# A fused attention and expert kernel: TensorE's order around the weighted values, and each value group cut into two halves of the queries

## The reference

```
x = x + attention(layernorm(x), ctx, ctx, length)     # 16 batches, x is [16, 128, 512]
    per head: attn = softmax(SCALE*log(length) * (q^T k)); out = attn v
x = x + experts(layernorm(x))                          # 2048 tokens of 512, 8 experts, 2 chosen
    per token: sum over the two chosen e of w_e * (silu(t w1_e) * (t w3_e)) w2_e
```

## Time and profile before

| | |
|---|---|
| three runs | 1285.31, 1286.80, 1287.75 us; median 1286.8 us |
| profiled execution | span 1285.3 us from first to last instruction; the page gives no other time of it |
| TensorE | 1125.7 us busy (88%) |
| VectorE | 590.4 us busy (46%) |
| ScalarE | 449.9 us busy (35%) |
| GpSimd | 606.7 us busy (47%) |

### The profile page before, as it was taken

How to read it: one execution, slowest core, us unless ns; L and a number is a source line. 1 busy time by engine, 2 the same in 40 slices (tenths; PEclk the granted TensorE clock), 3 DMA queues, 4 the chain that set the end, 5 groups by cost and what they waited for, 6 DMA issues and landing times.

```text
span 1285.3 us, 20411 instructions
## 1 busy us (share of the span) xinstructions
PE 1125.7 (88%) x5561; PEld 472.8 (37%) x5562; DVE 590.4 (46%) x884; ACT 449.9 (35%) x812; POOL 606.7 (47%) x547
## 2 busy tenths in 40 slices
PE   1899999999999999727999999999999999999810
PEld 0223333333333332213555554455455555544300
DVE  5877787877788875131222222222222222222245
ACT  3266666666666666611111111111111111111200
POOL 6434666666666541126504707428281473800045
PEclk9999999999999999958999999999999999999965
DMA  6454555555555441024203305124241333310157
GB/s 181 148 167 141 168 168 168 164 162 158 159 159 165 138 133 45 19 98 159 99 33 131 123 25 196 65 98 163 98 163 33 131 130 123 122 33 33 34 158 259
DMA packets 87243, 158.92 MB, mean 124 GB/s; under 512 B 13696, under 2 KB 52608, under 8 KB 81792
## 3 DMA queue, kind: packets, MB, share of 16 engines
q1 hardware_dynamic: 73728, 90.23, 22.9%
q0 software_dynamic: 12896, 67.12, 14.9%
q10 hardware_dynamic: 576, 1.05, 0.2%
HBM read 107.50 MB, written 50.86 MB: 123 GB/s over the span
## 4 chain that ended last, share of the span: by engine, by line
PE 75%; DVE 8%; DMA 6%; issue 5%; ACT 4%; POOL 2%; SPq 1%; DVEq 0%; POOLq 0%; ACTq 0%; PEldq 0%
PE rows L1048 30%; PE heads_out L1048 15%; PE heads_out L951 7%; PE scores L938 6%; PE rows L924 6%; ACT W L559 3%; DVE nm L682 3%; DMA W<-parts_dram 3%; PE scores L1081 2%; PE misc L1000 2%; DMA U<-expert_out_dram,fidx 1%; PE misc L1021 1%; PE misc L1040 1%; PE misc L977 1%; POOL U L523 1%
## 5 line engine op out<-in xcount | busy, mean ns | idle before, releaser
L1048 PE MATMUL rows<-W,U 128*128 x1776 | 392.1, 381 | 4.6 <-issue 3.0
L559 ACT ACTIVATE W<-scores 128x512 f32<-128x512 f32 x512 | 282.9, 598 | 160.2 <-PE scores L938 155.0
L682 DVE TENSOR_REDUCE nm<-rows 128x2 f32<-128x1024 f32 x256 | 305.5, 1220 | 58.3 <-PE rows L924 41.3
L1048 PEld LDWEIGHTS rows<-W,U 128*128 128x128 bf16 x1776 | 174.5, 98 | 208.9 <-issue 9.7
L1048 PE MATMUL heads_out<-W,U 128*128 x888 | 200.3, 383 | 5.2 <-issue 5.1
L924 PE MATMUL rows<-W,U 96*128 96x512 bf16 x512 | 163.7, 404 | 44.8 <-DMA W<-parts_dram 25.8
L865 DVE TENSOR_TENSOR U<-rows,U 128x512 f32<-128x512 f32 x78 | 53.8, 691 | 318.9 <-ACT U L627 318.9
L938 PE MATMUL scores<-U,W 128*128 128x512 bf16 x512 | 180.3, 387 | 13.9 <-ACT W L559 4.8
L400 POOL TENSOR_TENSOR W<-U,W 128x2048 bf16<-128x2048 f32 x42 | 171.0, 4072 | 7.7 <-POOL W L399 7.7
L627 ACT ACTIVATE U<-rows 128x512 f32<-128x512 f32 x78 | 46.4, 598 | 331.0 <-PE rows L1048 329.9
L951 PE MATMUL heads_out<-W,U 128*32 128x512 f32 x1024 | 138.0, 611 | 0.1
(11 more groups left out here) (144 smaller groups left out, 780.5 us busy)
## 6 DMA issues: line engine op xcount, KB each, us to landing
U<-wpack_dram POOLq DMA_DIRECT2D x42, 1024.0 KB, 5.2
parts_dram<-U SPq DMA_DIRECT2D x32, 384.0 KB, 4.1
U<-parts_dram SPq DMA_DIRECT2D x32, 384.0 KB, 3.9
W<-parts_dram SPq DMA_DIRECT2D x32, 384.0 KB, 5.1
U<-slots_dram SPq DMA_DIRECT2D x39, 256.0 KB, 2.6
expert_out_dram<-U SPq DMA_DIRECT2D x39, 256.0 KB, 2.1
parts_dram<-U SPq DMA_DIRECT2D x32, 256.0 KB, 3.9
stage<-wpack_dram POOLq DMA_DIRECT2D x12, 512.0 KB, 5.3
```

What stands on the lines that cost most here:

```text
L559: s.activation(probs[:, w % 2, j, kk, :], sc[u % 2][:, :], ACT.Exp) \
L682: v.tensor_reduce(nm[:, bb.parity, 2 * k:2 * k + 2], p1[k % 2][:, :].rearrange("p (c k) -> p c k", c=2), AX_X, ALU.max, negate=True).then_ ...
L1048: ins = m.matmul(bank, stat[:, s_part, k, :], W[:, bass.ds(at_w, 512)], start=(k == 0 and n == 0), stop=(k == n_chunks - 1 and n == 2))
```

## The change

`values` takes a fourth argument `qh` and does 256 of the 512 queries: four matmuls of 256 columns. Each former call is two now, and each loads the same stationary blocks. `pv_done` is raised by the second half alone. TensorE's order in half a window is now: score, unit, score, first half of the values, score, unit, score, second half. The small products are at new places between them, and `take_out` stands at other places among ScalarE's exponentials. VectorE writes one more small table (`tile_at`, twice, once in the whole program), whose first column is -1 in place of 0, and one comparison for the expert tiles reads that.

```diff
-                exps(0, range(0, 3))
+                exps(0, range(0, 4))
                 if pv2.within(0, B - 1):      # copies zt
...
-                exps(0, range(3, 6))
+                exps(0, range(4, 8))
+                exps(1, range(0, 1))
                 if pv.within(0, B - 1):
                     take_out(pv, 1)
-                exps(0, range(6, 8))
+                exps(1, range(1, 2))
...
-                exps(1, range(0, 4))
+                exps(1, range(2, 6))
...
-                exps(1, range(4, 8))
-                exps(2, range(6))
+                exps(1, range(6, 8))
+                exps(2, range(8))
+                exps(3, range(0, 1))
                 if full:
                     take_out(b, 0)
-                exps(2, range(6, 8))
-                exps(3, range(0, 5))
+                exps(3, range(1, 5))
...
+                st.step(v.tensor_copy(tile_at[:, :], tio[:, 1, 0:B]))
+                st.step(v.memset(tile_at[:, 0:1], -1.0))
...
-                def values(bb, w, kk):
+                def values(bb, w, kk, qh):
...
+                    cols = slice(256 * qh, 256 * qh + 256)
...
                     for j in range(4):
-                        ins = m.matmul(ob[32 * j:32 * j + 32, :], vt[:, bb.parity, kc, 4 * (w // 2) + j, :],
-                                       probs[:, w % 2, j, kk, :], start=(kc == 0), stop=(kc == 3))
-                    if kk == 1:
+                        ins = m.matmul(ob[32 * j:32 * j + 32, cols], vt[:, bb.parity, kc, 4 * (w // 2) + j, :],
+                                       probs[:, w % 2, j, kk, cols], start=(kc == 0 and qh == 0),
+                                       stop=(kc == 3 and qh == 1))
+                    if kk == 1 and qh == 1:
                         ins.then_inc(S["pv_done"], 1)
...
                 for w in range(4):
-                    for u in range(8):
-                        if u % 2 == 0:
-                            rows_unit(4 * w + u // 2)
+                    for part in range(2):
+                        u = 4 * part
                         if full:
                             score(w, u)
...
+                        rows_unit(4 * w + 2 * part)
+                        if full:
+                            score(w, u + 1)
+                        if (w, part) == (0, 1) and routes:
+                            reader = gates()
+                        if (w, part) == (1, 0) and ahead:
+                            reader = turn_v()
+                        if (w, part) == (1, 1) and behind:
+                            reader = pick_heads()
+                        value_half(w, part, 0)
+                        if full:
+                            score(w, u + 2)
+                        rows_unit(4 * w + 2 * part + 1)
+                        if (w, part) == (3, 0) and ahead:
+                            reader = turn_maxima()
+                        if full:
+                            score(w, u + 3)
+                        if (w, part) == (0, 0) and routes:
+                            reader = turn_z()
+                        if (w, part) == (1, 1) and routes:
+                            reader = ranks()
+                        if (w, part) == (3, 0) and behind:
+                            reader = spread_sums()
+                        value_half(w, part, 1)
```

More of the change, by code:

```diff
@@ L157, in build @@
         tio = sb("tio", [P, 2, T + 1], F32)
+        tile_at = sb("tile_at", [P, B], F32)
         upto = sb("upto", [P, E, E], F32)
@@ L813, in _ @@
             link(v.tensor_tensor(k3, cnt.unsqueeze(2).to_broadcast([P, E, B]),
[L814 removed]
+                                 tile_at[:, :].unsqueeze(1).to_broadcast([P, E, B]), ALU.is_gt))
             link(v.tensor_reduce(tiles, k3, AX_X, ALU.add))
@@ L958, in slot, with turn_z, gates @@
                     (S["m_ready"], b.n + 1) if full else None
+                def turn_z():
+                    pe.wait_ge(S["z_ready"], b.n - 1)
+                    pe.wait_ge(*reader)
+                    for k in range(KD):
+                        ins = m.transpose(misc[:, k * P:(k + 1) * P], z[:, b.parity, k * P:(k + 1) * P], ident[:, :])
+                    ins.then_inc(S["zt_ps"], 1)
+                    return S["zt_ready"], b.n - 1
+                def gates():
+                    pe.wait_ge(*reader)
+                    for k in range(KD):
+                        ins = m.matmul(misc[:, 0:E], zt[:, k, :], gw[:, k, :], start=(k == 0), stop=(k == KD - 1))
+                    ins.then_inc(S["gate_ready"], 1)
+                    return S["gate_used"], b.n - 1
@@ new lines, in turn_v, with pick_heads @@
+                def turn_v():
+                    pe.wait_ge(S["cv_in"], b.n * 16 + 32)
+                    if reader:
+                        pe.wait_ge(*reader)
+                    for kc in range(4):
+                        ins = m.transpose(misc[:, kc * P:(kc + 1) * P], cv[:, kc * P:(kc + 1) * P], ident[:, :])
+                    ins.then_inc(S["vt_ps"], 1)
+                    return S["vt_ready"], b.n + 2
+                def pick_heads():
+                    if reader:
+                        pe.wait_ge(*reader)
+                    pe.wait_ge(S["og_ready"], b.n * 2)
+                    for gr in range(2):
+                        ins = m.matmul(misc[:, :], selu[:, gr, :], og[:, gr, :], start=(gr == 0), stop=(gr == 1))
+                    ins.then_inc(S["u_ready"], 1)
+                    return S["us_ready"], b.n
@@ new lines, in ranks, with turn_maxima @@
+                def ranks():
+                    pe.wait_ge(*reader)
+                    pe.wait_ge(S["mask_ready"], b.n - 1)
+                    m.matmul(misc[:, 0:E], ltri[:, :], maskb[:, :], start=True, stop=False)
+                    m.matmul(misc[:, 0:E], onesb[:, :], mask_sum[:, :], start=False, stop=True) \
+                        .then_inc(S["rank_ready"], 1)
+                    return S["rank_used"], b.n - 1
+                def turn_maxima():
+                    pe.wait_ge(S["p1_used"], b.n * 16 + 32)
+                    if reader:
+                        pe.wait_ge(*reader)
+                    m.transpose(misc[:, 0:P], nm[:, nb.parity, :], ident[:, :]).then_inc(S["mt_ready"], 1)
+                    return S["m_ready"], b.n + 2
@@ new lines, in spread_sums, with value_half @@
+                def spread_sums():
+                    pe.wait_ge(S["rec_in"], b.n * 16)
+                    if reader:
+                        pe.wait_ge(*reader)
+                    m.matmul(misc[:, :], selb[:, :], r8[:, :], start=True, stop=True).then_inc(S["r_ready"], 1)
+                    return S["t_ready"], b.n
+                routes = pv2.within(0, B - 1)
+                def value_half(w, part, qh):
+                    if w == 0 and behind:
+                        values(pv, 3, part, qh)
+                    if w > 0 and full:
+                        values(b, w - 1, part, qh)
```

64 lines of the change are left out of this document (3 added, 61 removed).

## The result

The kernel after takes 1313.76 us (median of four runs, 1312.35 to 1316.07) against 1287.28 for before (1285.31 to 1289.91): a ratio of 1.0204, interval 1.0182 to 1.0225, slower by 26.5 us. The forecast was 1312. One run further down, of dve_late_old, came out slow (1308.94 us, granted clock 0.914 against 0.96 in the others) and its median leaves that run out.

The account below looks back on a forecast made before the run. It took TensorE (busy 88% of the span) as the bound, with a round trip of two score banks adding to it. Parts 1 to 6 summed as 31 - 36 + 13 + 10 + 12 - 4 = +26, 1312 us, range 1300 to 1325.

Parts of the forecast that it names:

- part 1: Values on TensorE: 128 more groups, each paying a fixed 0.24 us, +31 us.
- part 2: Scores on TensorE: waits for ScalarE's exponentials go in the new order, -36 us.
- part 3: Half groups and transposes wait for ScalarE's later copy out of heads_out, 0.64 and 0.20 us each, +13 us.
- part 4: Shared bank misc: the spread sums wait 0.70 us for VectorE to split the maxima, 14 batches, +10 us.
- part 5: Window 3's last score waits 0.88 us for an exponential behind ScalarE's store of xres, 14 batches, +12 us.
- part 6: The unit's wait for reloaded stacked keys goes, -4 us; the routing's long wait stays at about 1.1 us.
- Rival B: Values: a second group costs nothing fixed, halves take 0.55 us; +4 us in all, 1291 us, 8 in 100.
- rival C: Values: short groups cost more, 0.77 us a half; 1328 us, 12 in 100.
- the chain: Later rival account: a batch lasts one round through several engines; a removed wait returns unless the order shortens that round.
- the ledger: How the prediction was worked: each new TensorE wait costs what its row shows, and they add up.
- Rival A: New waits for heads_out, misc and the store don't last to TensorE: -9 us, 1278 us, 5 in 100.
- Rival D: Transfers of stacked queries and keys set the period, TensorE's order doesn't matter: 1287 us, 3 in 100.

Follow-up runs that it names:

- dve_late_old: Kernel before, with VectorE's small routing steps between the maxima of three units instead of together ahead of them: 1281.86 us, ratio 0.9948.
- order_full: Kernel after's order, but whole values groups of 512 columns at the first half's place and nothing at the second's: 1313.01 us, ratio 1.0204.
- split_old: Kernel before in its old order, each values group cut into two adjacent halves of 256 columns: 1296.93 us, ratio 1.0062.
- e_spread: Kernel after, with the spread sums (L1018) behind the second half group instead of ahead of it: 1317.12 us, ratio 1.0227.
- e_store: Kernel after, with ScalarE's store of xres behind all exponentials of window 3: 1314.51 us, ratio 1.0212.
- late_new_cs: Kernel after, with copies out of heads_out earlier, the xres store behind window 3's exponentials and VectorE's routing steps further back: 1296.94 us, ratio 1.0075.
- dve_late_new: Kernel after, with VectorE's small routing steps between the maxima of three units instead of together ahead of them: 1308.28 us, ratio 1.0157.

## Why the prediction came out right, and where its steps did not

The parts, measured by distances between starts and as means a batch (the forecast's batch from its own terms; a plus is time added):

| part | forecast | measured |
|---|---|---|
| 1, twice as many groups | 1.92 | 1.76 |
| 2, waits for exponentials | -2.4 | -2.08 |
| 3, the copies out of heads_out | 0.84 | 0.76 |
| 4, L1018 behind VectorE | 0.70 | 0.66 |
| 5, the store of xres | 0.88 | 0.92 |
| 6, the reload | -0.32 | -0.06 |
| 6, the routing's hold | 0 | 0.14 |
| small products, by difference | 0 | -0.23 |
| period | 1.62 | 1.87 |

**The split (part 1, +31).** The size was right: a pair takes 2 x (0.09 + 0.57) = 1.32, 1.34 forecast, 1.10 before. As the cause of the loss it was not: order_full has no split and is as slow. The 0.24 is paid for the change of the array's mode and not for loads. Rival B (0.43 to the next start) and rival C (0.77 a half) both fall, with 0.57 to the next start and 0.31 ahead. That stationary operands are loaded ahead did not hide it.

**Waits for exponentials (part 2, -36).** They went from the plain parts: 3.08, as forecast. They were priced too high, since the 0.23 of the plain part was put on all 121 and the mean is about 0.20: 2.08 a batch and not 2.4, some 5 us in 14 batches. The last two distances lost 1.5, where 3 was forecast for the last batch. What is left (33.1 in 58 waits on the load queue) lies in windows where a hold bunches TensorE's work. This gain and part 1's cost belong together: split_old (+9.6 for the split in the old order) and order_full (+5.74 for it in the first 13 distances of the new order, -6.06 in the last two) show it from both sides.

**The copy out of heads_out (part 3, +13).** 0.64 and 0.20 were forecast; the means are 0.56 in window 3 and 0.20 in window 1. In the batch shown it is 0.50 (268.20 to 269.01, less the 0.31 of a free half group) and 0.15 (285.34 to 286.02, less the 0.53 of free transposes). This is the one new wait whose removal pays (9 us).

**L1018 behind VectorE (part 4, +10).** 0.70 forecast, 0.66 in the mean, 0.71 in the batch shown (270.35 to 271.37, less 0.31, which L1018 takes behind a score where nothing holds it, in the last batch but one). Its own price is none: in e_spread it is gone and the time stays.

**The store (part 5, +12).** 0.88 forecast, 0.92 in the mean, 0.99 in the batch shown. Its own price is none too (e_store).

**The reload (part 6, -4).** It hardly went: the first unit of window 3 is held 0.22 a batch in before and 0.16 in after, and the 0.32 of the one batch of the earlier trace rows was put on twelve. So it is -0.06 a batch, under 1 us in all. The routing's hold was taken as unchanged at 1.1; it is 1.05 before and 1.19 after, which is +2.

**The sum.** Parts 3 to 5 are waits that the trace shows at nearly the forecast size, and +26 came out as +26.5. That it fits to half a us is luck. The forecast is 14 batches of 1.62, 22.7 us, and 3 more at the edges; measured, 14 batches of 1.87 make 26.2 and leave next to nothing for the edges. In the batch itself the gains of part 2 and of the reload were 0.58 too large and the hold took 0.14 more, while the other parts and the small products took 0.47 less. What failed is the step "parts 3 to 5 add": parts 4 and 5 are places where TensorE waits for a chain that is late anyway, and take nothing away with them when they go (0 us for each, where 10 and 12 stood). By the chain the same number reads as the stages of the table above. The prediction could have seen this: z's end comes 7.8 after the spread sums in both kernels (266.43 less 258.59, 279.20 less 271.37), and everything up to there is fixed by L1018, which makes that wait's position, not its length, the thing to price. That the sum was right all the same is no proof of the ledger: TensorE's idle time and its work together are the period by definition, so a ledger with about the right sizes must sum about right; it can't say what to remove.

Rival A (1278) fell where it said it would: the copy wasn't done when TensorE reached the half group. Rival D (transfers, 1287) fell with the period. One reading was off besides: the profile of before was put to the run of 1285.31; the run of after with span 1310.8 took 1312.35, 1.5 around its span, so before's span of 1285.3 belongs to about 1286.8, and the sum against the profiled execution would have been 1313.

The 4.2 ahead of the first spread sums are no more than 0.4 the tile table's: VectorE's two steps for it stand at 30.8 to 32.0, and the first score starts at 53.98 before and 54.36 after. The other 3.8 come in the first batches' own windows.

```profile
53.98 1.06 PE L938 MATMUL scores<-U,W 128*128 128x512 bf16 x2
```

```profile
54.36 0.59 PE L942 MATMUL scores<-U,W 128*128 128x512 bf16 x1
```

What stays open: late_new_cs, with the new order's waits mended, is still 10 us above before, and no run takes the split out of it.

## What to carry to other kernels

When stages of several engines chase each other round a loop, price a new order along that loop: where it starts the loop's first instruction, and what lies between the meetings. A list of TensorE's waits gives the right total and the wrong remedies; before a wait is called a cost, look whether the next meeting has slack (here: does z end just before its reader starts?). Look at the granted clock behind a wait that grew, too. A group of matmuls in another tiling mode pays at its two edges, so it may be cut in pieces side by side at no cost to TensorE (look when the reader of the result starts, it was later in split_old), and pays for each piece that stands alone.

## What the runs showed of the hardware that I had not expected

**A subtract on GpSimd.** tensor_scalar over 128x512 fp32 with two operands per partition took 2076 ns as (subtract, mult) and 761 ns as (add, mult), 11 times each. The subtracted scalar stood in another tile than the added one, so the operator is not shown to be the only cause.

**Tiny VectorE steps beside GpSimd.** Steps over 8 columns or 2, which take 0.16 to 0.17 elsewhere in the same kernel, took 1.06 and 0.99 when they fell beside an operation of GpSimd, and ended with it. Timeline of dve_late_old, VectorE then GpSimd:

```profile
270.90 0.17 DVE L703 CAST experts<-order 128x2 uint32 x1
...
274.20 1.06 DVE L710 TENSOR_TENSOR maskb<-masks 128x8 bf16<-128x8 f32 x1
...
300.82 0.99 DVE L701 COPY scores<-sorted 128x2 f32 x1
```

```profile
273.35 1.90 POOL L397 TENSOR_TENSOR W<-stage,zero 128x1024 f32 x1 [0.44 <-POOL U L400]
...
300.63 1.16 POOL L400 TENSOR_TENSOR rest<-norm,U 128x512 f32<-128x512 f32 x1 [0.19 <-POOL U L399]
```

274.20 + 1.06 is 275.26, and 273.35 + 1.90 is 275.25; 300.82 + 0.99 is 301.81, and 300.63 + 1.16 is 301.79. The Trainium skill (SBUF — State Buffer, Who interferes with whom) has it that a VectorE instruction with two SBUF inputs contends with a GpSimd instruction that reads SBUF, and that in a two-port mode, which a copy can enter, the one that comes second waits for the other's whole instruction. The ends agree: L710 has two inputs in SBUF, and L701 is a copy, though in which mode it ran the trace doesn't say. Whether this ate part of the 12 to 17 us that I had expected of dve_late_new was not measured by itself.
